# A two-layer graph network on one core: the edge loops go from items of 512 edges to units of two 256-edge halves

## What is computed

```
h = relu(layernorm(x))
f_src, f_v, f_dst = h @ W_src.T + b_src, h @ W_v.T + b_v, h @ W_dst.T + b_dst
e   = leaky_relu(f_src[src] + f_dst[dst])          # 106250 x 128
sa  = exp(e - segment_max(e, dst)[dst]) / segment_sum(...)[dst]
x   = x + segment_sum(f_v[src] * sa, dst)
h   = relu(layernorm(x))
s   = silu(silu(edge_attr_32 @ fc1 + b1) @ fc2 + b2) @ fc3 + b3
msg = silu(h[src] @ W_node * s + edge_attr_16 @ W_sh)
a   = silu(silu([h[src,:64], h[dst,:64], edge_attr_32] @ aW1 + ab1) @ aW2 + ab2) @ aW3 + ab3
alpha = softmax(a, over all edges).mean(heads)
x   = x + layernorm(h + segment_sum(msg * alpha, dst) @ W_out)
```

## Time and profile before

| what | us |
|---|---|
| median of 3 runs | 3500.36 |
| lowest, highest | 3499.36, 3505.07 |
| the profiled execution, span from first to last instruction | 3499.8 |
| layer 0 edges (first to last L987) | 173.4 to 1520.9 |
| layer 1 edges (first to last L1402) | 1710.9 to 3077.3 |
| aggregate (first to last L1609) | 3111.8 to 3437.8 |

### The profile page before, as it was taken

How to read it: one execution, slowest core, us unless ns; L and a number is a source line. 1 busy time by engine, 2 the same in 40 slices (tenths; PEclk the granted TensorE clock), 3 DMA queues, 4 the chain that set the end, 5 groups by cost and what they waited for, 6 DMA issues and landing times. The chain is left out here.

```text
span 3499.8 us, 76247 instructions
## 1 busy us (share of the span) xinstructions
PE 2791.7 (80%) x17156; PEld 1977.5 (57%) x17380; DVE 2528.0 (72%) x4445; ACT 2041.3 (58%) x4527; POOL 2085.4 (60%) x2160
## 2 busy tenths in 40 slices
PE   1577777777777777744799999999999999958885
PEld 0355555555555555532466666666666666647774
DVE  5699999999999999996345555555554555567776
ACT  6355555555555555545355555555555555568885
POOL 0177777777777777732777777777777777500001
PEclk9899999999999999978899999999999999989997
DMA  2555444554444444413777777777777777647662
GB/s 71 172 143 145 142 142 141 142 144 144 142 139 141 143 141 143 141 34 106 206 218 222 218 218 221 220 218 221 217 222 220 220 220 218 190 132 202 202 202 82
DMA packets 391734, 595.68 MB, mean 170 GB/s; under 512 B 73317, under 2 KB 237855, under 8 KB 391682
## 3 DMA queue, kind: packets, MB, share of 16 engines
q0 software_dynamic: 98304, 268.57, 27.1%
q1 hardware_dynamic: 242626, 247.55, 25.4%
q10 hardware_dynamic: 50752, 78.99, 6.6%
HBM read 501.15 MB, written 93.68 MB: 170 GB/s over the span
## 5 line engine op out<-in xcount | busy, mean ns | idle before, releaser
L1194 POOL DMA_INDIRECT l_G<-rows_d,l_sidx x1024 | 1002.5, 979 | 363.1 <-issue 276.3
L807 POOL DMA_INDIRECT l_G<-rows_d,l_sidx x1024 | 1014.0, 990 | 330.5 <-issue 305.0
L1322 ACT ACTIVATE l_h<-l_H,l_cols 128x512 f32<-128x512 f32 x512 | 350.7, 685 | 557.3 <-PE l_H L1229 540.5
L875 PE MATMUL l_accp<-l_we,l_ohe 128*128 128x256 f32 x2048 | 486.3, 380 | 0.0
L831 PE MATMUL l_A<-ident,l_G 128*128 128x128 f32 x1024 | 172.8, 293 | 380.6 <-DVE l_oht L978 323.0
L1386 DVE TENSOR_TENSOR big<-l_SC,l_b 128x512 f32<-128x512 f32 x256 | 177.1, 692 | 387.9 <-PE l_SC L1258 387.9
L875 PEld LDWEIGHTS l_accp<-l_we,l_ohe 128*128 128x128 f32 x2048 | 371.1, 191 | 40.1
L831 PEld LDWEIGHTS l_A<-ident,l_G 128*128 128x128 f32 x1024 | 111.2, 144 | 482.0 <-issue 243.5
L1258 PEld LDWEIGHTS l_SC<-big,l_h 128*128 128x128 f32 x2048 | 263.6, 191 | 146.8 <-issue 146.8
L1548 PE MATMUL ag_accp<-ag_msg,ag_pick 128*128 128x128 f32 x2048 | 286.5, 288 | 73.7 <-ACT ag_msg L1532 32.9
L903 ACT ACTIVATE l_qe<-l_A 128x512 f32<-128x512 f32 x256 | 153.3, 599 | 325.8 <-PE l_A L834 209.7
(11 more groups left out here) (182 smaller groups left out, 5755.4 us busy)
## 6 DMA issues: line engine op xcount, KB each, us to landing
msg_d<-l_msg ACTq DMA_DIRECT2D x256, 256.0 KB, 2.2
ag_msg<-msg_d SPq DMA_DIRECT2D x256, 256.0 KB, 2.9
l_G<-rows_d,l_sidx POOLq DMA_INDIRECT x2048, 3.3
l_lo<-mark_d SPq DMA_DIRECT2D x256, 128.0 KB, 3.0
l_lo<-code_d SPq DMA_DIRECT2D x256, 128.0 KB
l_in<-in_ea_dram SPq DMA_DIRECT2D x512, 64.0 KB
l_fd<-dst_d SPq DMA_DIRECT2D x256, 96.0 KB, 3.4
l_pd<-dst_d SPq DMA_DIRECT2D x256, 96.0 KB
```

The lines of the kernel that those rows point to most:

```text
L807: nc.gpsimd.indirect_dma_start(out=G[:, s, j, :], out_offset=None, in_=rows_d[0][:, :], in_offset=bass.IndirectOffsetOnAxis(ap=sidx[:, hal ...
L875: last = nc.tensor.matmul(accp[b][:, 0:2 * C], oh_e[:, b, j, :], we_t[:, b, j, :], start=(j == 0), stop=(j == TJ - 1), skip_group_check=True)
L1194: nc.gpsimd.indirect_dma_start(out=G[:, s, j, :], out_offset=None, in_=rows_d[1][:, :], in_offset=bass.IndirectOffsetOnAxis(ap=sidx[:, hal ...
L1322: nc.scalar.activation(out_t[:, s % 2, :], in_p[:, :], ACT.Silu, bias=cols[:, col:col + 1]).then_inc(ready, 1)
```

## The change

A unit takes the place of an item. It has two halves of 256 edges (`HT`), each with a chunk and a block of its own. The number of halves is (106250 + 49 x 255) // 256 = 463, so `NI` is 232 units of 512 edge places. Everything that belongs to one block is done once for each half: two values of `items_row` become four on SP, each load is made for each half, one-hots are built and block sums are added for each half.

- Layer 0: the one-hot product is issued for each half (6 matmuls of 256 columns for 3 of 512). The sums become feature-major: `we_t` is now the stationary operand, the one-hot the moving one (8 matmuls of 128 columns for 4 of 256, and the turned column of L872 is gone). The rescaling then touches the one node at the front of the unit, whose place is read from the new `front_row`: 2 columns for 256. `rest_of` and its ACT instruction are gone. `add` is called twice.
- `node_tables`: PE turns the quotients back, DVE adds them to X, in place of POOL.
- Layer 1: five loads for an item become three for each half; the attributes come as one load of 80 rows from `ea_d`, a joined copy which ACT's queue makes in memory by five DMAs at the end of `prepare` (5 x 16 rows of 106752 numbers, 34.2 MB); layer 1 starts when they are done. `pd_t` has 4 buffers for 8.
- Aggregate: the sum is taken for each half, and `add` is called twice in a step.
- `prepare`: tables, choice matmuls and index copies for halves, and `fronts()` on DVE.

```diff
+HT = IT // 2
+NH = (E + NB * (HT - 1)) // HT
+NI = -(-NH // 2)
...
+                        for k in range(JOINS):
+                            rows = ea16 if k == JOINS - 1 else ea32[k * SH % EA:k * SH % EA + SH, :]
+                            act.dma_start(ea_d[k * SH:(k + 1) * SH, :].rearrange("a (k e) -> (a k) e", e=EQ),
+                                          rows.rearrange("a (k e) -> (a k) e", e=EQ)).then_inc(joined, 16)
```

In layer 0 on PE:

```diff
-                            nc.tensor.matmul(accp[b][:, 2 * C:3 * C], w_t[:, g, 0:1].to_broadcast([P, P]), ident[:, :],
-                                             is_transpose=True, start=True, stop=True, skip_group_check=True)
-                            for j in range(TJ):
-                                last = nc.tensor.matmul(accp[b][:, 0:2 * C], oh_e[:, b, j, :], we_t[:, b, j, :],
+                            for h in range(2):
+                                for k in range(2):
+                                    for j in range(HJ):
+                                        last = nc.tensor.matmul(accp[b][:, h, k, :], we_t[:, b, h * HJ + j, k * C:(k + 1) * C],
+                                                                oh_e[:, b, h * HJ + j, :], start=(j == 0), stop=(j == HJ - 1),
```

In layer 0 on DVE:

```diff
+                            at = dve.value_load(front_row[0:1, bass.ds(i, 1)], min_val=0, max_val=NP - 1)
+                            mine = acc0[:, :, bass.ds(at, 1)]
+                            dve.wait_ge(w_ready, i + 1)
+                            if after(i, 1):
+                                dve.wait_ge(acc_done, 2 * i)
+                            nc.vector.tensor_scalar(mine, mine, w_t[:, g, 0:1], None, ALU.mult).then_inc(acc_scaled, 1)
...
                         def step(lap, u):
                             leaky(lap, u, 1)
-                            mine = scale(lap, u, -2)
+                            scale(lap, u, -2)
                             running(lap, u, 1)
-                            add(lap, u, -2, mine)
+                            add(lap, u, -2, 0)
                             back(lap, u, 1)
+                            add(lap, u, -2, 1)
```

In layer 1 on SP:

```diff
-                            for t in (OF_H, OF_A):
-                                sp.dma_start(in_t[t, s, :], ea32[:, bass.ds(off, IT)]).then_inc(ld[s], 16)
-                            sp.dma_start(in_t[OF_SH, s, :], ea16[:, bass.ds(off, IT)]).then_inc(ld[s], 16)
+                            for h in range(2):
+                                half = slice(h * HT, (h + 1) * HT)
+                                sp.dma_start(lo_t[:, s, half], code_d[bass.ds(off[h], HT)].partition_broadcast(P)).then_inc(ld[s], 16)
+                                sp.dma_start(pd_t[:, s % R, h, :], dst_d[1][bass.ds(row[h], P), :]).then_inc(ld[s], 16)
+                                sp.dma_start(in_t[:, s, half], ea_d[:, bass.ds(off[h], HT)]).then_inc(ld[s], 16)
```

In the aggregate on DVE:

```diff
                         def step(lap, u):
+                            add(lap, u, 0, 0)
                             weigh(lap, u, 2)
-                            add(lap, u, 0)
+                            add(lap, u, 0, 1)
```

More of the change, by code:

```diff
@@ L667, in _, with back @@
                     def _(pe):
+                        def back(q):
+                            for g in pairs(q):
+                                if g % PAIRS == 0:
+                                    pe.wait_ge(s_quotient, q + 1)
+                                if g >= 2:
+                                    pe.wait_ge(s_sum, g - 1)
+                                for k in range(2):
+                                    last = nc.tensor.matmul(qt[g % 2][:, k, :], w[:, 2 * g + k, :], ident[:, :], is_transpose=True,
+                                                            start=(k == 0), stop=(k == 1), skip_group_check=True)
+                                last.then_inc(s_back, 1)
+                        back(0)
+                        back(1)
                         pe.wait_ge(s_in, 16)
```

341 lines of the change are left out of this document (184 added, 157 removed).

## The result

| | before | after |
|---|---|---|
| median (us) | 3500.85 (4 runs) | 3909.99 (4 runs) |
| lowest, highest | 3499.36, 3505.07 | 3906.95, 3912.64 |
| profiled execution, span | 3499.8 | 3905.1 |

The changed kernel is slower: the ratio of the times is 1.1164, with an interval of 1.1149 to 1.118. The forecast was slower too, but 3619 us, and its range ended at 3705.

What follows compares the result with a forecast made beforehand. It took DVE and POOL to bound layer 0, PE layer 1 (SP's queue next), and DVE's queue most of the aggregate. 3499.8 - 116 + 45 + 10 + 20 + 160 = 3619 us, range 3530 to 3705.

Steps and rivals of the forecast that it cites:

- The joins, +45: Start of layer 0: 34.2 MB of memory-to-memory copies partly delay the edge loop, +45 us.
- The joins hold the gathers up: Rival at layer 0's start: the copies delay the gathers, +120 to +150 us for +45, total 3694 to 3724; chance 0.14.
- a sign of being wrong: Start of layer 0: the prediction is wrong if the joins stop the edge loop outright.
- Layer 0, -116: Layer 0: 232 units at 5.33 us in place of 256 items at 5.284, -116 us (bounds -128 and -77).
- prepare and `node_tables`, +10: Both stages: DVE's 25 additions cost 8 us, `prepare` gets wider matmuls and `fronts()`; +10 us together.
- Layer 1, +20: Layer 1: SP's queue, with four fetches and six loads, sets 6.0 us a unit, +20 us.
- The other case, 5.70: Layer 1: if no stationary load were hidden, PE would need 5.70 us a unit for 5.38; no chance given.
- Aggregate, +160: Aggregate: two fetches back to back on DVE's queue bring a unit to 2.10 us, +160 us.
- the rival's 1.37 for a hidden fetch: Rival in the aggregate: DVE's second fetch is hidden, pitch 1.37 us, total 3450; chance 0.05.
- The sign given for it: Aggregate: a pitch near 2.1 us, with most of DVE's idle time ahead of L1667 put down to "issue".
- the joins in front: Start of layer 0: the case of copies delaying the gathers, total 3694 to 3724 us; chance 0.14.
- the last rival: Layer 1 and aggregate: neither SP's nor DVE's queue binds, total 3306 us, near the plain share 232 / 256; chance 0.05.

Runs made afterwards that it cites:

- e1_host_join: Changed kernel with the joined attributes laid out by the host as one input, the five copies and the wait for them gone: 3804.56 us.
- e9_head0: Changed kernel, no hint, with the first instruction of DVE's layer 0 loop placed on a multiple of 256 instructions: 3814.31 us.
- e3_l1_two_fetches: Changed kernel with SP in layer 1 fetching two values a unit for four, both halves loading from the same places, six loads kept: 3681.59 us.
- e4_agg_one_fetch: Changed kernel with the aggregate's second half added at the place fetched for the first, still two additions: 3733.19 us.
- e11_before_agg_fetch_twice: Kernel before, with DVE in the aggregate fetching an item's block twice and using the second value: 3650.41 us.

## Why the prediction was wrong, step by step

- **The joins, +45 (bounds 0 and +120): wrong in the choice.** They cost 105 (`e1_host_join`). "The joins hold the gathers up" was a rival at 0.14, and it is what happened, though not by way of ACT's queue, which was free after 3.38 us; "gathers are issued four items ahead" was no shelter, since at the start nothing is ahead yet. The profile's windows show the edge loop stopped outright from 200 to 250 us, which the prediction itself had named as a sign of being wrong. The Trainium skill, "DMA: Bandwidth & Descriptors", in the section on queues, rings and completion order, has a DMA engine take a packet of each queue in turn. The trace agrees: 324, 328 and 325 packets of the three queues from 200 to 250 us, of 15.59, 0.91 and 0.19 MB. The size of 53 KB given for the joins was right (53,376 bytes), that of 1 KB for a gather low (up to 4,096 bytes). The prediction had the mechanism and its dear end in hand, and took 45 against it, with no row that speaks for a start free of friction.
- **Layer 0, -116: the step that failed.** The settled step was sized rightly (5.35 for 5.33), but 232 x 5.855 - 1353 = +5. Not in the sum at all, neither as a term nor as a rival, was the 4.1 us that DVE's queue stands still at the branch, once a lap. `e9_head0` gives back 94 us within layer 0, and 232 x 5.448 - 1353 = -89 is what the step would have been worth. Most of the other 27 us are stops of about 3 us ahead of the instruction that takes a gather's rows (L1087 there, put down to "issue": 17.4 us in 6 stops from 500 to 1400 us, so some 24 in the layer by my estimate); the kernel before has the same kind, 32.3 us in 10. So the three fetches behind long instructions were covered, as foretold. I had read the work and the waits of each engine, and never how long a loop's code had become.
- **prepare and `node_tables`, +10 (bounds -5 and +25): low.** 16.4 + 7.7 = 24, at the upper bound.
- **Layer 1, +20 (bounds -73 and +66): right mechanism, too small.** SP bound it, at 6.31 us for 6.0, outside the bound of 6.2, so +92. The loads cost 3.0 us for 3.2; the four fetches, with holds and register work, 3.3 for 2.8. The mean TENSOR_LOAD is 0.349 us in the changed kernel, 0.270 in the kernel before and 0.271 in `e3_l1_two_fetches`: 4 x 0.08 = 0.3 us, about what the forecast missed. That PE would need 5.38 when fed is confirmed by two runs at 5.365. The other case, 5.70 with no load of a stationary operand hidden, didn't come about.
- **Aggregate, +160 (bounds +114 and +207): right.** +190; the pitch was 2.227 for 2.10. `e4_agg_one_fetch` and its converse both show the fetch on DVE's queue. With it gone two halves need 1.465 us a unit, so the rival's 1.37 for a hidden fetch was 0.1 low. The sign given for it held in part: of the idle time ahead of L1667 58.2 us are put down to "issue", but 121.8 to the sum before.
- **The sum.** 105 - 45 = 60 from the joins, 121 in layer 0 (less the 5 of them that are the copies' and stand in the 105), 72 in layer 1, 30 in the aggregate and 14 in the small parts are 292, for 3910 - 3619 = 291. All five terms came out too low, and one cost wasn't among them; the range of 3530 to 3705 had been drawn as if such errors cancelled, and it even ended inside the band of 3694 to 3724 that the prediction gave to the joins in front. That it would be slower was forecast for the right reason in layer 1 and in the aggregate, which make 279 of the 405 us between the spans. With the stall at the branch added and all else as forecast the sum would have been about 3715 (3619 + 96, `e9_head0`). One side remark was off as well: the 3306 us of the last rival isn't near the plain share, since 3499.8 x 232 / 256 is 3172.

What stays open: why SP's TENSOR_LOAD is at times two to four times its usual length in the changed kernel's layer 1, and not where PE sets the pace (of the 154 long ones 92% fall into PE's products at L1294 and L1298, of the others 34%, but all engines keep step with SP there, so this may be no more than a coincidence); and how the hint does away with the fetching instead of making it early. Neither was tried.

## What to carry to other kernels

Count the sequencers' work as an engine's: a register fetch of 0.6 to 0.75 us, once or more per step, decided stages whose steps are 1.3 and 5.4 us, and cost nothing in layer 0, where it stood behind long instructions. The cure was to lay the values of a step side by side and fetch them at once. When a change lengthens a hand-unrolled loop, look at the queue's rows at its closing branch for a gap of some 4 us and at the instruction packets in the DMA rows, and place or hint the loop. A bulk copy belongs in parts among the work and not ahead of the first loads of a stage, however much DMA time the stage leaves idle; compare the sizes of the packets, not only the bytes.

## What the runs showed of the hardware

- A TENSOR_LOAD on DVE's queue took 0.30 us for one value and 0.22 more for each further one up to three (0.52, 0.75), but 0.34 for four that begin at a multiple of four; SP took 0.30 for such four and 0.27 for one. The Trainium skill ("Runtime: NRT & Kernel Launch", "Instruction fetch mechanics") gives some 200 ns per register even in bulk, and the page speaks of registers loaded from HBM. The values here lie in a tile on the chip; the step of 0.22 from one to three of them is close to that figure, and the four are far below it.
- One more fetch of one value on DVE's queue lengthened the aggregate's step by 0.60 us (`e11_before_agg_fetch_twice`), twice the 0.30 of its TENSOR_LOAD.
- A taken branch back to the head of a loop that touches three blocks of 256 instructions stopped DVE's queue for 3.9 to 4.4 us each turn, about 95 us in 26 and in 29 turns. The length alone (300 instructions) cost 0.3 us a turn where it touched two. A hint at the head removed both the gap and the packets.
- The same 34.2 MB cost 105 us in one lump, in packets of 53 KB, and 4 to 6 us in 29 parts, in packets of 15 KB. Beside the lump three queues got 324, 328 and 325 packets through in 50 us, whatever their size.
